# A four-layer graph network on one core: node tiles placed in mirrored order when the front half of the edge chunks meets more buckets, and a look-up list of 2080 entries in place of 3248

## The chip, the core and the metric

The program runs on one core of one Trainium2 chip. The metric is the device time of one execution in microseconds (us). A core has TensorE (PE in the profile; its weight loads are listed apart as PEld), VectorE (DVE), ScalarE (ACT), GpSimd (POOL) and SyncE (SP). Each engine has a sequencer that takes its instructions in the order in which they are written; in the profile a q behind the engine's name (PEldq, DVEq, ACTq, SPq) marks what the sequencer itself does: waits, register work, issue of DMAs. Matmuls write to PSUM, which has eight banks of 512 fp32 columns per partition.

## What is computed

Four graph layers run on 6250 nodes with 128 features and 200,000 edges. Each takes h = relu(layernorm(x)) and adds its result to x:

```python
x = x + gin(h, ...)      # sums of h[src] by dst, then two linear layers
x = x + gat(h, ...)      # attention over the edges
x = x + sage(h, ...)     # three times: mean of h[src] by dst
x = x + meta(h, ...)     # the edge layer, below

def meta(x, edge_index, edge_attr, u, batch, W1a, b1a, W1b, b1b, W2a, b2a, W2b, b2b):
    row, col = edge_index
    h = concatenate([x[row], edge_attr], axis=1)
    h = relu(h @ W1a + b1a) @ W1b + b1b
    sums = segment_sum(h, col, n_nodes)
    agg = sums / clip(counts, 1.0)[:, None]
    z = concatenate([x, agg, u[batch]], axis=1)
    return relu(z @ W2a + b2a) @ W2b + b2b
```

The edges come sorted by dst; src is random. Both are inputs, so the program counts and sorts them itself.

## The kernel before

**Sizes.** Nodes lie in 49 tiles of 128. A bucket is a pair (dst tile, src tile): 49 x 49 = 2401. Edges are stored by bucket in chunks of 128, two chunks to a pair; each dst tile begins at a new pair. There is room for 832 pairs, 1664 chunks. Counted from the inputs, 807 pairs are filled, and 25 lie empty at the end.

**Stages in order.** A histogram of the buckets; a chain of small steps that each wait for the one before (`relay`), which turns it into positions; `place_and_scatter`, which computes each edge's row and writes it to the tensor `bucketed` in HBM; `build_adjacency`, which makes the 49 x 49 blocks of the count matrix; the GIN, GAT and three SAGE layers, which multiply with that matrix; `edge_pass`, for the meta layer; and the tail.

**The edge pass** (6919 to 8991 us) has two blocks. It needs relu(table[src] + edge term) for every edge, `table` being the node part of the first linear layer, and sums it by dst. The chunks are treated in two ways. The far half (the last 416 pairs) is gathered from HBM by POOL with indirect DMAs (L2082), two per pair. The near half (the first 832 chunks) is looked up by TensorE from a copy of the table on chip: for every (chunk, src tile) that has edges, DVE makes a 128 x 128 one-hot matrix (L2220) and TensorE multiplies it with the tile of the table into the chunk's bank (L2161). This is one look-up. Both halves run interleaved in the first block: with each far pair go `PER_PAIR` = 8 look-ups. The list of look-ups has `LOOKS` = 3248 entries, a bound that holds for any graph; entries behind the last real look-up are dummies that add zeros to a bank nobody reads. Counted from the inputs, 3925 look-ups would serve all chunks, and 2021 of them fall in the near half.

**What sets the order in the first block.** DVE does per pair n: `message` (L2195), load of the chunk and tile numbers of the 8 look-ups into registers (L2210, L2212, TENSOR_LOAD), 8 one-hots (L2220), `rectify` (L2200), `add` for pair n-1 (L2206) and the scatter matrix of pair n+3 (L2188). TensorE's sequencer does per pair: the same two register loads (L2167, L2169), 8 look-ups (each a wait, two register operations, then the matmul, which is two weight loads and two matmuls in fp32), and the pair's own product (L2178), which waits for `rectify`. The one-hots have 8 buffers. ACT prepares each near chunk's bank with the edge term (`prepare`, L2114) and, when the chunk's look-ups are done, empties it with the relu (`evict`, L2121); there are four banks, so chunk c+4 is prepared after chunk c is emptied. After each four chunks ACT's sequencer issues three DMAs (L2145, L2098, L2103) and loads four registers (L2137). DVE waits for the bank (`s_clear`) at every second look-up. The second block (`near_pe`, L2274 and on) sums the near rows by dst and has no look-ups.

**The adjacency stage.** POOL reads `bucketed` back in 208 rounds of 8 chunks (L843, L847); every 16 rounds fill a chunk block, which TensorE turns (`turn`, L918); `find` (L927 to L930) picks the columns for 128 hits with selectors that DVE makes (L875), and the hits follow in runs of 16: DVE makes two one-hots each (L889, L890), TensorE multiplies (L942), ACT empties banks, SP stores blocks (L985).

## Time and profile before

| | us |
|---|---|
| median of 3 runs | 8997.42 (8996.03 to 9005.73) |
| the profiled execution | 9031.9 |
| its span | 9030.2 |

| engine | busy us | share | instructions |
|---|---|---|---|
| PE | 6296.6 | 70% | 36507 |
| PEld | 4249.3 | 47% | 36507 |
| DVE | 6360.5 | 70% | 17765 |
| ACT | 2836.5 | 31% | 6169 |
| POOL | 2691.6 | 30% | 2966 |

The shares are means over stages with different limits, so each stage has to be read by itself. PEclk is the clock that TensorE was granted: 1.00 is 2.4 GHz, 0.50 is 1.2 GHz. "Idle before" is what ended an engine's idle time; "issue" says that nothing in the profile shows what it waited for. A line number is that of the kernel's source.

### The profile page before, as it was taken

What the parts mean: (1) busy time and instruction counts of PE and PEld (TensorE: products, weight loads), DVE (VectorE), ACT (ScalarE), POOL (GpSimd) and SP (SyncE); (2) the same over time, 40 slices, a digit from 0 to 9 for tenths busy, and PEclk for the clock granted to TensorE, in tenths of its full rate; (3) what the DMA queues carried; (4) which work ended last, traced back from release to release, by engine and by line L of the source; (5) the groups of instructions that cost most, each with busy time, mean ns of one, the idle gap of its engine ahead of it and who ended that gap; (6) DMA issues with size and microseconds to landing.
All of it is one profiled execution on the core that took longest, in us unless ns stands there. A gap on an engine that the chain in (4) does not pass through costs nothing. (4 is left out here: it accounts for less than half of the span.)

```text
span 9030.2 us, 137943 instructions
## 1 busy us (share of the span) xinstructions
PE 6296.6 (70%) x36507; PEld 4249.3 (47%) x36507; DVE 6360.5 (70%) x17765; ACT 2836.5 (31%) x6169; POOL 2691.6 (30%) x2966
## 2 busy tenths in 40 slices
PE   4767777777555666566501788599997777777779
PEld 3545555555312222222201777444445666666668
DVE  6777777777668999655588999611024777777778
ACT  0222222222245776344400788300001333320000
POOL 0666767766646200000000000000002444444430
PEclk9666666666667999799855999799999999999999
DMA  2333333333498555699597666276676776752256
GB/s 98 94 96 95 97 97 97 96 97 97 127 393 270 163 169 145 227 337 329 163 387 311 207 215 213 95 245 217 215 251 178 180 183 179 181 144 63 63 105 194
DMA packets 1048196, 1605.78 MB, mean 178 GB/s; under 512 B 111567, under 2 KB 699236, under 8 KB 1033906
## 3 DMA queue, kind: packets, MB, share of 16 engines
q1 hardware_dynamic: 761756, 1179.89, 41.4%
q0 software_dynamic: 111328, 277.62, 9.5%
q10 hardware_dynamic: 174394, 139.51, 5.8%
q8 instruction: 351, 5.75, 0.3%
q14 instruction: 367, 3.01, 0.1%
HBM read 1177.49 MB, written 419.08 MB: 177 GB/s over the span
## 5 line engine op out<-in xcount | busy, mean ns | idle before, releaser
L774 POOL DMA_INDIRECT bucketed<-arena,wide x1563 | 1527.1, 977 | 882.6 <-issue 850.6
L2161 PE MATMUL psum<-wide,arena 128*128 x6496 | 1210.4, 329 | 397.5 <-DVE arena L2220 391.5
L2161 PEld LDWEIGHTS psum<-wide,arena 128*128 128x128 f32 x6496 | 989.2, 195 | 616.9 <-issue 491.8
L2220 DVE TENSOR_SCALAR arena<-wide,tile_first 128x128 f32 x3248 | 871.4, 302 | 469.4 <-PE psum L2161 289.8
L2082 POOL DMA_INDIRECT arena<-table,src_i x832 | 802.0, 964 | 1006.9 <-PE psum L2178 870.8
L942 PE MATMUL psum<-arena 128*128 128x512 bf16 x2304 | 705.8, 444 | 425.5 <-DVE arena L890 247.4
L662 PE MATMUL psum<-w_edge,arena 128*128 128x256 f32 x1568 | 869.7, 655 | 0.0
L890 DVE TENSOR_SCALAR arena<-sums 128x512 bf16<-128x512 int16 x2304 | 821.1, 356 | 0.0
L691 ACT CAST wide<-psum 49x49 f16<-49x49 f32 x1568 | 310.8, 198 | 1556.0 <-PE psum L669 893.9
L2030 POOL DMA_DIRECT2D table<-wide x13 | 9.6, 736 | 2478.5 <-DVE wide L1929 2478.5
L1686 PE MATMUL psum<-sums,arena 128*128 128x129 f32 x4802 | 602.3, 281 | 154.3 <-DVE arena L1676 154.3
L889 DVE TENSOR_SCALAR arena<-sums 128x128 bf16<-128x128 int16 x2304 | 599.3, 260 | 123.4 <-PE psum L942 122.3
L942 PEld LDWEIGHTS psum<-arena 128*128 128x128 bf16 x2304 | 241.2, 105 | 884.0 <-issue 723.8
L1686 PEld LDWEIGHTS psum<-sums,arena 128*128 128x128 f32 x4802 | 556.0, 192 | 200.7 <-DVE arena L1676 200.7
L1869 PE MATMUL psum<-arena,h 128*128 128x512 f16 (+1 forms) x2548 | 561.0, 371 | 43.9 <-DMA arena<-halved 42.4
L1370 DVE SCALAR_TENSOR_TENSOR arena<-arena 128x1536 f16<-128x1536 f32 (+2 forms) x245 | 359.0, 1465 | 312.6 <-ACT arena L1335 273.9
L669 PE MATMUL psum<-arena 128*113 128x177 bf16 x1568 | 546.4, 348 | 0.0
L968 ACT COPY wide<-psum 128x512 f32<-128x512 f32 x637 | 370.7, 582 | 472.3 <-PE psum L942 303.7
L1276 PE MATMUL psum<-arena,h 128*128 128x512 f16 (+1 forms) x1274 | 331.5, 398 | 248.7 <-ACT arena L1335 248.3
L1638 ACT ACTIVATE arena<-wide,s_a_mild 128x1280 f32<-128x1280 f32 (+1 forms) x245 | 326.8, 1334 | 439.8 <-PEq L103 439.8
L1335 ACT ACTIVATE arena<-arena 128x1536 f16<-128x1536 f32 (+2 forms) x245 | 305.6, 1248 | 434.9 <-DMA arena<-adjacency 415.0
L2121 ACT ACTIVATE arena<-psum 128x128 f32<-128x128 f32 x832 | 229.5, 276 | 670.1 <-PE psum L2161 562.6
(475 smaller groups left out, 12384.7 us busy)
## 6 DMA issues: line engine op xcount, KB each, us to landing
arena<-halved SPq DMA_DIRECT2D x441, 384.0 KB
arena<-adjacency SPq DMA_DIRECT2D x98, 1568.0 KB, 7.8
adjacency<-wide SPq DMA_DIRECT2D x588, 256.0 KB, 2.3
arena<-adjacency SPq DMA_DIRECT2D x196, 640.0 KB, 3.9
arena<-adjacency SPq DMA_DIRECT2D x147, 768.0 KB, 6.8
arena<-bucketed POOLq DMA_DIRECT2D x208, 528.0 KB, 6.1
halved<-arena SPq DMA_DIRECT2D x147, 384.0 KB, 6.3
wide<-bucketed ACTq DMA_DIRECT2D x208, 256.0 KB
```

The lines of the kernel that those rows point to most:

```text
L662: e.matmul(terms(k, c), lhsT=attr[k][:, at:at + P], rhs=W["edge"][:, :, :].rearrange("p c n -> p (c n)"), start=True, stop=True)
L669: update = e.matmul(psum[0:SPAN, 0, 0:TILES + P], lhsT=hot[k][:, c, by_dst], rhs=hot[k][:, c, by_both], start=False, stop=True, skip_group ...
L774: e.indirect_dma_start(bucketed, bass.IndirectOffsetOnAxis(ap=places[k][0:size, c:c + 1], axis=0), rows[k][0:size, c, :], None).then_inc(s ...
L889: e.tensor_scalar(hot_src[:, k, :], from_one[:, 0:P], row_of[:, ds(i * RUN + k, 1)], None, op0=ALU.is_equal)
L890: e.tensor_scalar(hot_key[:, k, :], from_one[:, 0:GROUP * P], key_of[:, ds(i * RUN + k, 1)], None, op0=ALU.is_equal).then_inc(s_ready, 1)
L942: e.matmul(flat[:, ds((bucket[k] & (BANKS - 1)) * 512, 512)], lhsT=hot_src[:, k, :], rhs=hot_key[:, k, :], start=False, stop=True, skip_gr ...
L968: e.copy(stage[:, k, :], psum[:, k, :]).then_inc(s_staged, 1)
L1686: last = e.matmul(psum[:, 4 * (r % 2) + c // 3, 129 * (c % 3):129 * (c % 3) + 129], lhsT=slots[n % 4][:, c * P:(c + 1) * P], rhs=node_rhs( ...
L1869: last = e.matmul(psum[:, 4 * (p % 2) + j, 0:width], lhsT=nodes[:, q, w, :], rhs=pieces[n % 4][:, 512 * j:512 * j + width], start=q == 0 a ...
L2082: e.indirect_dma_start(ring[:, k, c, :], None, table, bass.IndirectOffsetOnAxis(ap=src_i[:, chunk:chunk + 1], axis=0)).then_inc(s_got[k], 16)
L2161: e.matmul(flat[:, ds((chunk & 3) * 512 + 2048, P)], lhsT=hot[:, i % 8, :], rhs=table_in[:, ds(tile * P, P)], start=False, stop=True, skip ...
L2220: e.tensor_scalar(hot[:, i % 8, :], rows[:, ds((chunk[k] & 15) * P, P)], tile_first[:, ds(tile[k], 1)], None, op0=ALU.is_equal).then_inc(l ...
```

## The change

After the histogram, 35 more small steps count how many look-ups the near half would have. If it has more than half of all, tile t takes the place of tile 48 - t (`turn_round`, `swap`), and the empty pairs (`lead`, 25 here) lie ahead of the first edge instead of behind the last. The larger half is then far, and the list can be shorter for any graph: `LOOKS` is 2080, and `PER_PAIR` is 5, so all 416 far pairs carry look-ups (before 406). With the given inputs the comparison is 2 x 2021 > 3925, the tiles are mirrored, and the near half has 1906 look-ups; its first 50 chunks are empty. The counts are exact, since they are whole numbers made from the inputs.

Around this, `fill_spare` also blanks the first 112 chunks; `find` looks at one chunk block more, since the columns may lie up to 50 chunks later, so that two blocks are turned before the first `find`; SP reads the column of each block it stores from registers; ends of empty chunks are held at 1 or above.

```diff
-LOOKS = -(-(NEAR + BUCKETS_49 + 2) // 16) * 16
+MOST_LOOKS = (2 * (N_EDGES // (PAIR * P) + TILES) + BUCKETS_49 - TILES) // 2 + TILES
+LOOKS = -(-(MOST_LOOKS + 2) // 80) * 80
-PER_PAIR = 8
+PER_PAIR = 5
+LEAD = -(-2 * (PAIRS - N_EDGES // (PAIR * P)) // 16) * 16
...
             e.dma_start(bucketed_v[:, SPARE:CHUNKS, :]...).then_inc(s_empty, 16)
+            e.dma_start(bucketed_v[:, 0:LEAD, :].rearrange("p (r c) w -> p r (c w)", c=16),
+                        empty.rearrange("p c w -> p (c w)").unsqueeze(1).broadcast_to([P, LEAD // 16, 16 * EDGE_ROW])
+                        ).then_inc(s_empty, 16)
...
-                e.wait_ge(s_empty, 16)
+                e.wait_ge(s_empty, 32)
...
+        which_half = [
...
+            ("vector", lambda e, _: e.scalar_tensor_tensor(turn_round, both_sums[:, 1:2], 2.0, both_sums[:, 0:1], ALU.mult, ALU.is_gt), 1),
+            ("vector", lambda e, _: e.tensor_tensor(lead, lead, turn_round, ALU.mult), 1),
...
+            ("vector", lambda e, _: e.tensor_scalar(swap, iota[0:TILES, 0:TILES], row_to, None, op0=ALU.is_equal), 1),
...
+            ("tensor", lambda e, _: e.matmul(psum[0:TILES, 1, 0:TILES], lhsT=swap, rhs=hist, start=True, stop=True), 1),
+            ("vector", lambda e, _: e.tensor_copy(hist, psum[0:TILES, 1, 0:TILES]), 1),
+        ]
+        positions = which_half + [
...
             def chunk_blocks(b):
-                return [m for m in range(b - LAG, b + 1) if 0 <= m < CHUNK_BLOCKS]
+                return [m for m in range(b - LAG, b + 2) if 0 <= m < CHUNK_BLOCKS]
...
                     turn(0)
+                    turn(1)
                     find(0)
                     for b in range(BLOCKS):
                         batches(b, 0, 2)
                         if b + 1 < BLOCKS:
-                            turn(b + 1)
+                            turn(b + 2)
...
                     def store_blocks(i, rows):
+                        _, column = nc.values_load_multi_w_load_instructions(
+                            tile_column[:, i * BANKS:i * BANKS + rows], engines=(ENG.SP,), ...)
...
-                            e.dma_start(adj[:, g * GROUP:g * GROUP + w, ds(i * (BANKS * P) + (b // GROUPS) * P, P)],
+                            e.dma_start(adj[:, g * GROUP:g * GROUP + w, ds(column[b // GROUPS], P)],
...
                     e.sem_inc(s_clear, 15)
+                    e.sem_inc(s_looked, 1)
...
                             if k % 2 == 0:
-                                e.wait_ge(s_clear, chunk[k + 1])
-                                if i >= 8:
-                                    e.wait_ge(s_looked, i - 6)
+                                e.wait_ge(s_clear, chunk[min(k + 1, PER_PAIR - 1)])
+                                if i >= 7:
+                                    e.wait_ge(s_looked, i - 5)
```

DVE in the first block of the edge pass, the end of one pair. Before, the last two of eight look-ups share one wait, and `rectify` (L2200) follows:

```order
L2220 REGISTER_ALU [waits near_looked,near_clear]
L2220 ISA
L2220 TENSOR_SCALAR arena<-wide,tile_first 128x128
L2220 REGISTER_ALU
L2220 ISA
L2220 TENSOR_SCALAR arena<-wide,tile_first 128x128
L2200 TENSOR_SCALAR arena<-arena 128x256 [waits meta_sum]
```

Now the fifth and last look-up has a wait of its own, and `rectify` is L2260:

```order
L2280 REGISTER_ALU
L2280 ISA
L2280 TENSOR_SCALAR arena<-wide,tile_first 128x128
L2280 REGISTER_ALU [waits near_looked,near_clear]
L2280 ISA
L2280 TENSOR_SCALAR arena<-wide,tile_first 128x128
L2260 TENSOR_SCALAR arena<-arena 128x256 [waits meta_sum]
```

A pair has three one-hots fewer on DVE, and three look-ups fewer on TensorE, between the same neighbours; waits per pair go from four to three.

TensorE at the start of the adjacency stage. Before, one chunk block is turned (L918), then the first `find` (L927 to L930):

```order
L909 MATMUL psum<-blank 128x512 x4
L918 MATMUL psum<-ident,h 128x128 [waits s_cols]
L918 MATMUL psum<-ident,h 128x128 x2
L927 MATMUL psum<-wide 128x128 [waits s_picks]
L928 MATMUL psum<-wide 128x128
L930 MATMUL psum<-wide 128x128
L935 TENSOR_LOAD wide
```

Now two (L972), and `find` is L981 to L984:

```order
L963 MATMUL psum<-blank 128x512 x4
L972 MATMUL psum<-ident,h 128x128 [waits s_cols]
L972 MATMUL psum<-ident,h 128x128 x2
L972 MATMUL psum<-ident,h 128x128 [waits s_turned,s_cols]
L972 MATMUL psum<-ident,h 128x128 x2
L981 MATMUL psum<-wide 128x128 [waits s_picks]
L982 MATMUL psum<-wide 128x128
L981 MATMUL psum<-wide 128x128
L982 MATMUL psum<-wide 128x128
L984 MATMUL psum<-wide 128x128 x2
L989 TENSOR_LOAD wide
```

The first run of hits, behind the register load of L935 (now L989), stands behind a second wait for POOL's columns.

## Rows read from the trace of the kernel before

**Rows 1.** Two stretches: us, busy (xinstructions) of PE, PEld, DVE, ACT, POOL, PEclk, DMA, GB/s.

```profile
7300.00:7500.00 200.00, 156.34 (x899) 132.24 (x899) 145.60 (x538) 79.64 (x299) 85.03 (x91) 0.96 0.70 182
8300.00:8500.00 200.00, 159.31 (x946) 133.59 (x946) 151.29 (x567) 0.00 (x0) 90.45 (x94) 1.00 0.25 64
```

**Rows 2.** By line, 8100 to 8500 us: xcount | busy us, mean ns | idle before.

```profile
L2161 PE MATMUL psum<-wide,arena 128*128 x1514 | 277.2, 324 | 81.3 <-DVE arena L2220 80.9
...
L2220 DVE TENSOR_SCALAR arena<-wide,tile_first 128x128 f32 x757 | 200.3, 294 | 97.7 <-PE psum L2161 72.1 <-issue 10.6
L2082 POOL DMA_INDIRECT arena<-table,src_i x189 | 181.5, 961 | 218.2 <-PE psum L2178 188.9 <-issue 29.3
```

**Rows 3.** The same view, 7100 to 7500 us.

```profile
L2161 PE MATMUL psum<-wide,arena 128*128 x1427 | 267.1, 330 | 91.2 <-DVE arena L2220 89.2 <-issue 1.1
...
L2220 DVE TENSOR_SCALAR arena<-wide,tile_first 128x128 f32 x715 | 193.9, 306 | 109.1 <-PE psum L2161 60.8 <-ACT psum L2114 36.2 <-issue 4.9
```

**Rows 4.** Weight loads (PEld) in order of time: start us, us, what.

```profile
8305.06 0.53 PEld L2178 LDWEIGHTS psum<-arena 128*128 128x128 f32 x4
8306.64 2.67 PEld L2161 LDWEIGHTS psum<-wide,arena 128*128 128x128 f32 x16 [1.05 <-issue]
```

**Rows 5.** DVE in order of time, same columns, one pair.

```profile
8306.14 0.29 DVE L2200 TENSOR_SCALAR arena<-arena 128x256 f32<-128x256 f32 x1
...
8307.92 1.09 DVE L2220 TENSOR_SCALAR arena<-wide,tile_first 128x128 f32 x4 [0.62 <-PE psum L2161]
```

**Rows 6.** Register loads by line: xcount, ns min/median/max, first and last start.

```profile
L2167 PEldq TENSOR_LOAD <-wide x406: 587/592/1307, 6921.3 to 8711.9; - x136
...
L2137 ACTq TENSOR_LOAD <-src_i x208: 307/314/657, 6928.7 to 8062.4; - x104
...
L935 PEldq TENSOR_LOAD <-wide x144: 1101/1560/3655, 2471.1 to 3624.5; - x144
```

**Rows 7.** ACT around the end of four chunks, in order of time.

```profile
7161.79 0.28 ACT L2121 ACTIVATE arena<-psum 128x128 f32<-128x128 f32 x1 [0.43 <-PE psum L2161]
...
7164.03 0.28 ACT L2121 ACTIVATE arena<-psum 128x128 f32<-128x128 f32 x1 [1.66 <-issue]
```

**Rows 8.** Weight loads in a stretch at the lower clock, in order of time.

```profile
7182.04 3.39 PEld L2161 LDWEIGHTS psum<-wide,arena 128*128 128x128 f32 x16 [1.71 <-issue]
...
7186.33 2.67 PEld L2161 LDWEIGHTS psum<-wide,arena 128*128 128x128 f32 x16
```

**Rows 9.** Lines of the edge pass: xcount, ns min/median/max, first and last start us.

```profile
L2220 DVE TENSOR_SCALAR arena<-wide,tile_first x3248: 272/286/529, 6932.4 to 8712.9; 128x128 f32 x192
...
L2121 ACT ACTIVATE arena<-psum x832: 268/277/278, 6934.3 to 8066.7; 128x128 f32<-128x128 f32 x167
...
L2206 DVE TENSOR_TENSOR h<-h,psum x416: 267/280/289, 6938.2 to 8731.7; 128x128 f32 x139
```

**Rows 10.** Column copies of the adjacency stage, the same columns.

```profile
L843 POOL COPY h<-arena x208: 221/236/535, 2445.7 to 2820.9; 128x24 f32<-128x24 f32 x104
```

**Rows 11.** POOL at the start of the adjacency stage, in order of time.

```profile
2445.67 0.22 POOL L843 COPY h<-arena 128x24 f32<-128x24 f32 x1 [1.96 <-DMA arena<-bucketed]
...
2447.02 0.24 POOL L843 COPY h<-arena 128x24 f32<-128x24 f32 x1
```

**Rows 12.** Rows by line, 2426 to 2822 us, then 2822 to 3632 us.

```profile
L942 PE MATMUL psum<-arena 128*128 128x512 bf16 x476 | 187.6, 553 | 147.1 <-ACT psum L970 118.3 <-DVE arena L890 27.5 <-issue 0.9
...
L942 PE MATMUL psum<-arena 128*128 128x512 bf16 x1828 | 518.1, 415 | 278.5 <-DVE arena L890 219.9 <-ACT psum L970 51.3 <-issue 4.2
```

**Rows 13.** The chain of small steps before the scatter, in order of time.

```profile
153.66 0.14 DVE L419 CAST wide<-wide 49x1 f32<-49x1 int32 x1
...
155.42 0.14 DVE L427 TENSOR_SCALAR wide<-wide 49x1 f32<-49x1 f32 x1
...
156.80 24.11 SPq L411 DMA_DIRECT2D bucketed<-sums  x28
...
180.96 0.77 SPq L510 DMA_DIRECT2D hit_ends<-wide  x1
```

More of the change, by code:

```diff
@@ L413, in fill_last @@
             return emit
-        positions = [
+        first_i, final_i, next_i = (spread49[k].bitcast(i32) for k in (1, 2, 3))
+        filled, looks, looks_in, looks_at, flag, more_in = (spread49[k] for k in (4, 5, 6, 7, 8, 9))
+        swap = spread49[10]
+        both_looks, both_sums = spread49[11][:, 0:2], spread49[11][:, 2:4]
+        turn_round, lead, mirror, row_to, column_by, column_from = (spread49[12][:, k:k + 1] for k in range(6))
+        tile_column = sb("tile_column", [1, TILES], i32)
+        which_half = [
             ("vector", hist_wait, 1),
@@ L420, in build @@
             ("tensor", lambda e, _: e.matmul(psum[0:TILES, 1, 0:1], lhsT=before[0:TILES, 0:TILES], rhs=n_pairs, start=True, stop=True), 1),
-            ("vector", lambda e, _: e.tensor_copy(pair_at, psum[0:TILES, 1, 0:1]), 1),
+            ("tensor", lambda e, _: e.matmul(psum[0:TILES, 2, 0:1], lhsT=ones[0:TILES, 0:TILES], rhs=n_pairs, start=True, stop=True), 1),
+            ("vector", lambda e, _: e.tensor_scalar(pair_at256, psum[0:TILES, 1, 0:1], float(PAIR * P), None, op0=ALU.mult), 1),
+            ("vector", lambda e, _: e.tensor_scalar(lead, psum[0:TILES, 2, 0:1], -1.0, float(PAIRS), op0=ALU.mult, op1=ALU.add), 1),
@@ new lines, in build @@
+            ("vector", lambda e, _: e.tensor_tensor_scan(incl, ones[0:TILES, 0:TILES], hist, 0.0, ALU.mult, ALU.add), 1),
+            ("vector", lambda e, _: e.tensor_scalar(ends, incl, pair_at256, None, op0=ALU.add), 1),
+            ("vector", lambda e, _: e.tensor_tensor(first_i, ends, hist, ALU.subtract), 1),
+            ("vector", lambda e, _: e.tensor_scalar(final_i, ends, -1.0, None, op0=ALU.add), 1),
+            ("vector", lambda e, _: e.tensor_single_scalar(first_i, first_i, 7, op=ALU.arith_shift_right), 1),
@@ new lines, in build @@
+            ("vector", lambda e, _: e.tensor_scalar(looks_at, final_i, float(NEAR - 1), 1.0, op0=ALU.min, op1=ALU.add), 1),
+            ("vector", lambda e, _: e.tensor_tensor(looks_at, looks_at, first_i, ALU.subtract), 1),
+            ("vector", lambda e, _: e.scalar_tensor_tensor(looks_at, looks_at, 0.0, filled, ALU.max, ALU.mult), 1),
+            ("vector", lambda e, _: e.tensor_reduce(both_looks[:, 1:2], looks_at, axis=AX.X, op=ALU.add), 1),
+            ("tensor", lambda e, _: e.matmul(psum[0:TILES, 1, 0:2], lhsT=ones[0:TILES, 0:TILES], rhs=both_looks, start=True, stop=True), 1),
@@ new lines, in build @@
+            ("vector", lambda e, _: e.tensor_single_scalar(tile_column[:, :], tile_column[:, :], 7, op=ALU.arith_shift_left), 1),
+            ("tensor", lambda e, _: e.matmul(psum[0:TILES, 1, 0:TILES], lhsT=swap, rhs=hist, start=True, stop=True), 1),
+            ("vector", lambda e, _: e.tensor_copy(hist, psum[0:TILES, 1, 0:TILES]), 1),
+        ]
+        positions = which_half + [
+            ("vector", lambda e, _: e.tensor_reduce(tot, hist, axis=AX.X, op=ALU.add), 1),
+            ("vector", lambda e, _: e.tensor_scalar(tot_i, tot, float(PAIR * P - 1), None, op0=ALU.add), 1),
+            ("vector", lambda e, _: e.tensor_single_scalar(tot_i, tot_i, 8, op=ALU.arith_shift_right), 1),
+            ("vector", lambda e, _: e.tensor_copy(n_pairs, tot_i), 1),
+            ("tensor", lambda e, _: e.matmul(psum[0:TILES, 1, 0:1], lhsT=before[0:TILES, 0:TILES], rhs=n_pairs, start=True, stop=True), 1),
+            ("vector", lambda e, _: e.tensor_scalar(pair_at, psum[0:TILES, 1, 0:1], lead, None, op0=ALU.add), 1),
@@ L814, in build_adjacency @@
             head = part(h, 0, 3 * CHUNKS).rearrange("p (w c) -> p w c", w=3)
-            picks = [part(wide2, 2 * HITS + 64 * m, 64).bitcast(bf16) for m in range(LAG + 1)]
+            picks = [part(wide2, 2 * HITS + 64 * m, 64).bitcast(bf16) for m in range(LAG + 2)]
             from_one = part(sums, 0, 256).bitcast(i16)
@@ L868, in turn_and_pick @@
                     def turn_and_pick(b):
[L869 to L871 removed]
+                        for m in ([0, 1] if b == 0 else [b + 1]):
+                            if m < CHUNK_BLOCKS:
+                                e.wait_ge(s_turn, m + 1)
+                                e.tensor_copy(turned[:, m, :, :].rearrange("p w n -> p (w n)"), psum[:, 4, 0:3 * P]).then_inc(s_turned, 1)
                         if b:
@@ L980, in store_blocks @@
                     def store_blocks(i, rows):
+                        _, column = nc.values_load_multi_w_load_instructions(
+                            tile_column[:, i * BANKS:i * BANKS + rows], engines=(ENG.SP,), min_val=0, max_val=(TILES - 1) * P,
+                            skip_runtime_bounds_check_because="first node of a tile, made by this program from the tile's number")
                         for b in range(rows * GROUPS):
```

40 lines of the change are left out of this document (27 added, 13 removed).

## The prediction

> **What bounds the kernel now.** I read the stages first, by the view that gives busy time per stretch, then the groups by line, the order in time, and single lines. The stage that the change cuts is the first block of the edge pass. Its first one-hot starts at 6932.4 us and its last `add` at 8731.7 [rows 9]: 1799.3 us, a fifth of the span. In two stretches of it, one with near chunks and one after the last of them, ACT is busy or not at all, and the DMA engines 0.70 or 0.25 [rows 1]; no engine is full in either, so something periodic sets the pace. The period follows from the one-hots: 757 in 400 us is 4.23 us for each pair of eight in the far-only stretch [rows 2], 715 in 400 us is 4.48 us in the near stretch [rows 3].
>
> The reader is to see the 4.23 us put together on TensorE: 16 weight loads for eight look-ups in 2.67 us, four for the pair's product in 0.53, and a gap of 1.05 us before the next look-up [rows 4], sum 4.25. The gap is "issue", and in it the sequencer loads the numbers of the next look-ups: 592 ns each [rows 6], two per pair. The idle time that the groups give to DVE's one-hot [rows 2] is the same gap: DVE is ahead and itself waits for TensorE. DVE's own chain is close behind: from `rectify` to the next pair's first one-hot 1.78 us [rows 5], mostly its two register loads, then eight one-hots at 0.27 us at least [rows 9]: 2.18; with a load of tile numbers in every eighth pair (0.6 / 8 = 0.07) 4.03 us. POOL needs two gathers of 0.96 us and two pauses of 29.3 us / 95, some 0.31 each [rows 2]: 2.54 us.
>
> **The steps in the first block.**
>
> Look-ups: five per pair, six weight loads fewer at 2.67 / 16 = 0.167: -1.00 us per pair on TensorE, and three one-hots, -0.82, on DVE.
>
> Register loads: five numbers each instead of eight. The rows have loads of four (L2137, 314 ns), of eight (L2167, 592) and of 16 (L935, 1101 at least) [rows 6], about 70 ns for each number, so five should take 0.38: -0.42 us for the two, on either engine. The bounds are no gain, and the four-number load's -0.56. I take -0.42, by the rows on both sides. The Trainium skill ("DMA: Bandwidth & Descriptors", Latency and other measured facts) gives a floor of about 600 ns for a `tensor_load`; the row of four numbers at 314 ns disagrees. By that rule the step would be worth nothing, which is a rival below.
>
> New floors: TensorE 4.23 - 1.00 - 0.42 = 2.81 us; DVE 1.36 + 5 x 0.27 + 0.07 = 2.78; POOL 2.54. Three chains now lie within 0.3 us, where TensorE had 0.2 on DVE and 1.7 on POOL.
>
> In the near stretch a pair took 0.25 us more. DVE waited 36.2 us for ACT's banks over 715 / 8 = 89 pairs, 0.41 each [rows 3]. With 5 look-ups, a pair meets 832 / 1906 x 5 = 2.18 chunks instead of 832 / 2021 x 8 = 3.29, so 0.27, and this no longer has cover on DVE: 2.78 + 0.27 = 3.05. TensorE with the same addition as before comes to 3.06. Two coupled chains with equal length and irregular waits lose something to each other; I add half of the 0.27 and take 3.20. The ends are 2.81 (all hidden) and 3.75 (below).
>
> Count: 1906 look-ups are 381.2 near pairs, 34.8 more carry dummies. 381.2 x 3.20 + 34.8 x 2.81 = 1317.6 us.
>
> Start: the 50 empty chunks now lie first. DVE's first one-hot waits for chunk 50's bank, which is prepared after chunk 46 is emptied, and DVE holds everything behind it: `rectify`, so TensorE's product, so POOL's buffers. ACT must walk through 46 evictions. The step over a boundary of four chunks takes 7164.03 - 7161.79 = 2.24 us [rows 7], the others twice a copy of about 0.27, 0.51 with the overlap, so 3 x 0.51 + 2.24 = 3.8 us for four chunks, and 11.5 x 3.8 = 43 us. Bounds: 25 if the boundaries were free, 62 at the near stretch's own 5.45 us for four chunks (4.48 x 4 / 3.29). The pairs without look-ups at the end (now none), which ran quicker, cost 3 us more at the very end at most. So the block takes 43 + 1318 + 3 = 1364 instead of 1799: -435.
>
> **The steps before it.** Positions: 35 more steps ahead of SP's fills. Seven steps, two of them through TensorE, take 155.42 - 153.66 = 1.76 us [rows 13], 0.25 each: +8.8. The five steps behind the fills are hidden: SP issues fills for 24.11 us and only then the list that the next stage waits for [rows 13]. The other fill, of 112 chunks, costs its issue, some +0.4; it lands long before it is waited for.
>
> Adjacency: the first `find` needs 16 more of POOL's rounds. Undisturbed, one takes 2447.02 - 2445.67 = 1.35 us [rows 11], so it comes 21.6 us later. But until the last round at 2820.9 [rows 10] loads and stores share the DMA engines: 192 rounds from 2467.3 on took 1.84 each, so 16 undisturbed rounds give back 16 x 0.49 = 7.8, and the rounds end at 2813. By then 434 hits are done (476 in 348 us, 0.731 each), not 476, and the other 1870 run at 808 / 1828 = 0.442 us [rows 12]: 827 us, end at 3640 instead of 3630, +10. Twelve more selectors on DVE, which sets the pace there, at about a 0.29 us one-hot: +3. The register work on SP costs nothing: its 49 x 13 = 637 stores in some 1150 us leave it idle. Bounds +5 and +25; I take +13.
>
> Sum: -435 + 8.8 + 0.4 + 13 = -413 us. The profiled execution took 9031.9 us, 34.5 more than the median 8997.42; the difference carries over, so 8997 - 413 = **8584 us** (profiled about 8619).
>
> **The clock.** In a stretch at the lower clock (0.5, 1.2 GHz) the 16 weight loads take 3.39 us, but the next look-ups follow without a gap, 7186.33 - 7182.04 = 4.29 us later [rows 8]: the register loads hide behind slower work, and the pair costs what it did. Now ten loads at 0.212 and a product of 0.90 make 3.02 us, more than 2.81: the clock begins to count. The Trainium skill ("TensorE: Matmul & The Clock Gate", HAM oscillation) says that regular waits between groups of matmuls throttle the clock again. Here the gap stays, with less work around it, but relative work (14 products per 2.81 us against 20 per 4.23) rises; the row of the far-only stretch shows 1.00 at 20 per 4.23, so I expect it held.
>
> **Rivals.**
> - Register loads do not shrink: 3.23 far, 3.48 near. 43 + 381.2 x 3.48 + 34.8 x 3.23 + 3 = 1485; -314 + 22 = -292: 8705 us. For: the bottom of the TENSOR_LOAD rows for eight is stiff at 587. Against: the rows of 4 and 16.
> - Each of ACT's boundaries shows: 2.24 - 0.51 = 1.73 us per four chunks, 0.94 per pair, 3.75 us near. 1573; -226 + 22: 8793 us. For: no cover on DVE. Against: eight buffers hold 4 us of look-ups.
> - The clock stays low: 3.02 far, 3.20 + 0.21 near. 1451; -326: 8671 us.
> - Everything hides behind TensorE's 2.81: 43 + 416 x 2.81 + 3 = 1215; -584 + 22: 8435 us.
> - The comparison does not fire: 2021 look-ups in 404.2 pairs, no empty chunks ahead; 1330; -469 + 22: 8550 us. Against: 2 x 2021 is above 3925.
> - Slower: DVE's wait for a bank covers the whole pair in three steps, and each pair falls on one of ACT's boundaries in full, 2.79 + 2.24 = 5.03 us. 2061; +262 + 22: 9281 us. It decides from a near pair of 4.29 us on. Against: a boundary comes once in 1.8 pairs, and before DVE lost 0.41 us to ACT, not 2.24.
>
> **How the numbers follow.** Forecast 0.50, loads unchanged 0.12, boundaries shown 0.11, low clock 0.08, all hidden 0.12, no mirroring 0.03, slower 0.04. The forecast's own range is 8510 to 8660. From 8470 to 8740 it takes in the unchanged loads and the low clock and half of the hidden case, and leaves out the boundaries and the slower case: two in ten. A measurement of this kernel tells 0.2%, 18 us, from no change. Only the slower case and what lies between it and 8793 can end there: faster 0.95, same 0.01, slower 0.04.
>
> **What would show it.** Register loads of L2227 and L2270 near 0.38 us; one-hots (L2280) x2080; pairs of 3.2 us while ACT works, 2.8 after; first one-hot some 43 us later after the block's start; the last hit of the adjacency stage about 20 us later than now; the clock above 0.9 in the block. It is wrong if DVE's waits for ACT rise above 0.5 us per pair, or POOL's gathers become what pairs wait for.

## The result and the profile after

The changed kernel is slower: **9091.78 us** (median of 4 runs, 9084.15 to 9104.1) against 8997.77 (4 runs, 8996.03 to 9005.73) of the kernel before beside it. The ratio is 1.0104, interval 1.0087 to 1.0122: about 1%, small but clear of the noise. The forecast was 8584, and faster. A run that lay more than 1.5% above the fastest of its kernel is left out of medians and ratios; there is one such run, in experiment 8.

The profiled execution took 9096.69 us (span 9095.0) where that of before took 9031.9: +64.8. The profile of before is of an execution 34 us above its median and that of the changed kernel of one 5 us above, so the differences between the two profiles below add up to 65 us, not to 94.

The two stretches of the edge pass's first block, in the view of busy time per stretch (us, then busy of PE, PEld, DVE, ACT, POOL with instructions, PEclk, DMA share, GB/s), one with near chunks and one behind the last of them:

```profile
7400.00:7800.00 400.00, 261.21 (x1281) 230.18 (x1280) 225.98 (x823) 103.49 (x382) 176.13 (x184) 0.75 0.52 139
8660.00:8790.00 130.00, 85.30 (x438) 74.35 (x437) 76.97 (x282) 0.00 (x0) 49.40 (x52) 0.80 0.20 52
```

Against [rows 1], in the near stretch TensorE, DVE and ACT are *less* busy (PE 65% instead of 78%, DVE 56% instead of 73%), POOL is about as busy (44% and 43%), the DMA share fell from 0.70 to 0.52, and the granted clock is 0.75 instead of 0.96. Something waits more. The groups by line for 7400 to 7800 us (xcount | busy us, mean ns | idle before):

```profile
L2221 PE MATMUL psum<-wide,arena 128*128 x913 | 199.1, 378 | 136.7 <-DVE arena L2280 116.7 <-issue 19.7
L2141 POOL DMA_INDIRECT arena<-table,src_i x184 | 176.5, 959 | 225.9 <-PE psum L2238 195.3 <-issue 30.5
L2221 PEld LDWEIGHTS psum<-wide,arena 128*128 128x128 f32 x912 | 166.6, 252 | 167.5 <-issue 158.4
L2280 DVE TENSOR_SCALAR arena<-wide,tile_first 128x128 f32 x459 | 126.1, 303 | 168.0 <-PE psum L2221 68.2 <-ACT psum L2173 68.0 <-issue 26.7
```

459 one-hots are 91.8 pairs in 400 us: **4.36 us** for a pair of five look-ups, where eight took 4.48 [rows 3]. Weight loads wait 158.4 us for "issue", 1.73 us per pair. In order of time, one pair of the far-only stretch and the start of the next (weight loads on TensorE, with DVE's one-hots between them):

```profile
8703.02 1.67 PEld L2221 LDWEIGHTS psum<-wide,arena 128*128 128x128 f32 x10 [2.35 <-issue]
...
8704.61 0.53 PEld L2238 LDWEIGHTS psum<-arena 128*128 128x128 f32 x4
...
8706.47 1.41 DVE L2280 TENSOR_SCALAR arena<-wide,tile_first 128x128 f32 x5 [1.69 <-issue]
...
8707.43 1.67 PEld L2221 LDWEIGHTS psum<-wide,arena 128*128 128x128 f32 x10 [2.30 <-issue]
```

The work is what was forecast: ten weight loads in 1.67 us (2.67 x 10 / 16) and a product in 0.53. The gap is not: 2.30 us where before it was 1.05 [rows 4]; the period is 8707.43 - 8703.02 = 4.41. What fills it are the register loads, by line with ns min/median/max (L2227 and L2229 TensorE, L2270 and L2272 DVE):

```profile
L2227 PEldq TENSOR_LOAD <-wide x416: 582/1235/2195, 6938.1 to 8792.2; - x139
...
L2229 PEldq TENSOR_LOAD <-arena x416: 582/1230/1988, 6938.7 to 8793.5; - x139
...
L2270 DVEq TENSOR_LOAD <-wide x416: 592/1184/1830, 6947.8 to 8790.5; - x139
...
L2272 DVEq TENSOR_LOAD <-arena x416: 582/1183/2118, 6948.4 to 8791.8; - x139
```

Five numbers take 1.23 us, twice what eight took [rows 6]. The shortest are 0.58, and they come at regular places. Four pairs in a row, L2229 in the same columns:

```profile
L2229 PEldq TENSOR_LOAD <-arena x1: 694/694/694, 8647.2 to 8647.2; - x1
...
L2229 PEldq TENSOR_LOAD <-arena x1: 1242/1242/1242, 8651.1 to 8651.1; - x1
...
L2229 PEldq TENSOR_LOAD <-arena x1: 1230/1230/1230, 8656.0 to 8656.0; - x1
...
L2229 PEldq TENSOR_LOAD <-arena x1: 1228/1228/1228, 8660.4 to 8660.4; - x1
```

In every fourth pair it is near 0.6 (583 and 590 ns in the next two such pairs), in the other three 1.23. Pair n's five numbers start at number 5n, which is a multiple of four (16 bytes) for every fourth n. 1.23 / 5 is 0.246 us for each number. The whole trace has the same order: of L2229's 416 loads the first of every four (start at a multiple of four) has a median of 0.590 us, and the others, which start one, two and three numbers behind such a multiple, 1.243, 1.230 and 1.230.

These rows show a second thing. Five numbers from a multiple of four took 0.59 us, what eight take [rows 6], and not the 0.38 that the prediction expected of five. So the length alone was priced wrong as well: the steps that the rows show are for four numbers (0.31 us), eight (0.59) and sixteen (1.10), and five cost as much as eight.

The profile of the kernel *before* has such lines too, which the prediction did not read: loads of seven and of thirteen numbers.

```profile
L407 SPq TENSOR_LOAD <-last_i x4: 1142/2264/2862, 155.5 to 174.0; - x4
L407 ACTq TENSOR_LOAD <-last_i x3: 1396/2877/2897, 160.9 to 174.1; - x3
...
L960 ACTq TENSOR_LOAD <-wide x49: 1018/3146/3952, 2441.0 to 3561.1; - x49
```

Thirteen numbers at a median of 3.15 us are 0.242 each, while sixteen from a multiple of sixteen took 1.10 at least [rows 6]. Loads of 7 and 13 at steps of 7 and 13 meet a multiple of four only once in four, as those of 5 do. Of the loads of thirteen every fourth took 1.02 to 1.61 us, the others 2.91 to 3.95. The loads of seven are few and point the same way only roughly: the two that start at a multiple of four took 1.14 and 1.40 us, the other five 1.74 to 2.90, where seven times 0.246 would be 1.72.

The other stages. The block's first one-hot and its last `add`, and the last eviction of a near chunk, as in [rows 9]:

```profile
L2280 DVE TENSOR_SCALAR arena<-wide,tile_first x2080: 273/286/528, 6988.8 to 8794.4; 128x128 f32 x190
...
L2180 ACT ACTIVATE arena<-psum x832: 270/278/280, 6945.9 to 8653.3; 128x128 f32<-128x128 f32 x167
...
L2266 DVE TENSOR_TENSOR h<-h,psum x416: 267/280/290, 6994.5 to 8798.6; 128x128 f32 x139
```

DVE at the start of the block, in order of time:

```profile
6947.74 0.42 DVE L2255 TENSOR_TENSOR arena<-arena 128x256 f32<-128x256 f32 x1 [3.93 <-DMA arena<-table,src_i]
6988.79 1.29 DVE L2280 TENSOR_SCALAR arena<-wide,tile_first 128x128 f32 x5 [40.62 <-ACT psum L2173]
```

The start costs 40.6 us, against 43 forecast. SP's issues at the very beginning, in order of time (first number the start, second the time the issue took):

```profile
43.36 0.42 SPq L304 DMA_DIRECT2D bucketed<-sums  x1
43.83 0.56 SPq L307 DMA_DIRECT2D bucketed<-sums  x1
44.43 13.39 SPq L310 DMA_DIRECT2D look_marks<-blank  x1
57.86 2.54 SPq L311 DMA_DIRECT2D chunk_marks<-blank  x1
```

The second fill (L307) costs 0.56 us to issue, as forecast, but the third DMA stands 13.39 us behind the two. Only then do SP and the casts of DVE go on, and the histogram starts at 68.1 us instead of 54.6. Lines of the adjacency stage and of POOL's column copies (the latter in [rows 10] before), and the scatter before it:

```profile
L827 POOL DMA_INDIRECT bucketed<-arena,wide x1563: 909/958/1208, 269.8 to 2439.4; - x196
...
L944 DVE TENSOR_SCALAR arena<-sums x2304: 333/344/4580, 2514.7 to 3665.7; 128x512 bf16<-128x512 int16 x192
...
L896 POOL COPY h<-arena x208: 222/236/569, 2461.1 to 2834.7; 128x24 f32<-128x24 f32 x104
```

Before, the same scatter ran from 246.4 to 2423.9 and the same hits from 2472.5 to 3629.9. So the delay against before is +23.4 us where the scatter starts, +15.5 where it ends, +35.8 at the last hit, +66.9 at the block's last `add` (8731.7 before), +64.8 at the end.

### The profile page after: what moved, and what is told of

It is laid out like the page before. It is cut to its first block and busy times, and to the rows that moved or that the text cites. A ratio compares the mean times of both kernels' runs of the same rounds, so it can differ in the third digit from the quotient of the medians.

```text
span 9095.0 us, 127306 instructions
## 1 busy us (share of the span) xinstructions
PE 6057.6 (67%) x34166; PEld 4109.2 (45%) x34219; DVE 6070.1 (67%) x16644; ACT 2844.1 (31%) x6169; POOL 2693.8 (30%) x2966
## 5 line engine op out<-in xcount | busy, mean ns | idle before, releaser
L2221 PE MATMUL psum<-wide,arena 128*128 x4160 | 907.4, 378 | 674.1 <-DVE arena L2280 598.6
L2221 PEld LDWEIGHTS psum<-wide,arena 128*128 128x128 f32 x4160 | 760.6, 253 | 815.0 <-issue 773.1
L2280 DVE TENSOR_SCALAR arena<-wide,tile_first 128x128 f32 x2080 | 569.9, 301 | 794.4 <-ACT psum L2173 328.1
L944 DVE TENSOR_SCALAR arena<-sums 128x512 bf16<-128x512 int16 x2304 | 799.4, 347 | 0.0
L943 DVE TENSOR_SCALAR arena<-sums 128x128 bf16<-128x128 int16 x2304 | 577.0, 250 | 119.7 <-PE psum L996 119.0
```

The source lines that it names most:

```text
L943: e.tensor_scalar(hot_src[:, k, :], from_one[:, 0:P], row_of[:, ds(i * RUN + k, 1)], None, op0=ALU.is_equal)
L944: e.tensor_scalar(hot_key[:, k, :], from_one[:, 0:GROUP * P], key_of[:, ds(i * RUN + k, 1)], None, op0=ALU.is_equal).then_inc(s_ready, 1)
L2221: e.matmul(flat[:, ds((chunk & 3) * 512 + 2048, P)], lhsT=hot[:, i % 8, :], rhs=table_in[:, ds(tile * P, P)], start=False, stop=True, skip ...
L2280: e.tensor_scalar(hot[:, i % 8, :], rows[:, ds((chunk[k] & 15) * P, P)], tile_first[:, ds(tile[k], 1)], None, op0=ALU.is_equal).then_inc(l ...
```

## The experiments

**Theory:** a register load costs what the rows of 4, 8 and 16 numbers show (0.31, 0.59, 1.10 us) only if its first number lies at a multiple of four; otherwise each number costs about 0.24 us (0.246 on TensorE, 0.237 on DVE, where five took 1.18). **Rivals:** the loads are slow because five is an odd count; or they are slow because the loop around them is, and the real loss is ACT's banks after the mirroring.

Where not said otherwise runs are from one chip on which the kernel before took 9003.95 us (7 runs); on two others it took 9611.67 and 9622.74, since the scatter runs slower there (2710 to 2800 us from its first to its last part instead of 2178), so each ratio is to runs of before taken beside it.

**1. Aligned loads in the changed kernel.** Same look-ups, loads of eight numbers from the multiple of four at or below 5n:

```
- here = slice(n * PER_PAIR, (n + 1) * PER_PAIR)
+ here = slice(n * PER_PAIR // 4 * 4, n * PER_PAIR // 4 * 4 + 8)
- look_up(n * PER_PAIR + k, chunk[k], tile[k])
+ look_up(n * PER_PAIR + k, chunk[n * PER_PAIR % 4 + k], tile[n * PER_PAIR % 4 + k])
```

> The changed kernel, but each register load of a pair's look-up numbers begins at a multiple of four numbers (16 bytes) and reads eight, of which five are used. Theory (start of the load): in the changed kernel a load of five took 0.59 us in every fourth pair, where it began at such a multiple, and 1.23 us in the other three; here all take 0.59. TensorE's floor per pair is then 4.23 - 1.00 = 3.23 us, near 3.5 to 3.6, far 3.25: block 43 + 381 x 3.55 + 35 x 3.25 = 1510 us instead of 1810, total about 8790 us, clock in the block back above 0.9. Rival (with five look-ups per pair ACT's bank boundaries and the low clock set the pace, the loads fill idle time): the total stays within 50 us of 9090.

Measured: **8672.69 us** (8669.75 to 8676.74), ratio 0.9633 (0.9617 to 0.9649): 419 us less than the changed kernel. Loads by line, then the stretch 7300 to 7700 us with near chunks and one behind the last of them, and the groups in the first:

```profile
L2227 PEldq TENSOR_LOAD <-wide x416: 587/591/1381, 6926.2 to 8369.4; - x139
```

```profile
7300.00:7700.00 400.00, 285.75 (x1664) 240.01 (x1662) 292.84 (x1070) 132.15 (x488) 229.05 (x238) 0.96 0.68 179
8280.00:8370.00 90.00, 65.14 (x392) 54.12 (x392) 67.16 (x248) 0.00 (x0) 41.79 (x44) 1.00 0.23 63
```

```profile
L2221 PE MATMUL psum<-wide,arena 128*128 x1188 | 229.5, 332 | 114.2 <-DVE arena L2281 104.6 <-issue 8.9
...
L2281 DVE TENSOR_SCALAR arena<-wide,tile_first 128x128 f32 x595 | 163.8, 304 | 103.1 <-PE psum L2221 70.2 <-ACT psum L2173 19.1 <-issue 7.8
```

595 / 5 = 119 pairs: **3.36 us** each, 1.00 less, with the mirroring and its empty chunks still in place. Theory: three loads of 1.23 and one of 0.59 average 1.07, 0.48 more than 0.59; two per pair are 0.96, times 416 = 400 us. 419 were measured. The 8790 expected were 117 us too many: the expectation set a new block with its start in it (1510) against an old one without it (1810), and priced a near pair at 3.55 us where 3.37 came, (8260.5 - 6976.6) / 381.2. DVE's wait for ACT's banks fell from 68.0 / 91.8 = 0.74 us per pair to 19.1 / 119 = 0.16, so it was a consequence. The clock was one too: 0.75 went to 0.96 in the near stretch and 0.80 to 1.00 in the far one. Of the 1.00 us, (199.1 + 80.8) / 91.8 - (229.5 + 77.1) / 119 = 0.47 is TensorE's busy time, at the lower clock before (80.8 and 77.1 are its product, L2238, in the two stretches) and 136.7 / 91.8 - 114.2 / 119 = 0.53 its idle time. The two together are one cause seen twice: with the loads short, both go.

**2. The kernel before with both lists one number later.** Eight look-ups and loads of eight, nothing of the change, but each list starts 4 bytes further on. The two parts behind the list in `wide` move up by 16 numbers (64 bytes), which is not shown:

```
- tile_of = room(LOOKS).bitcast(i32)[0:1, :]
- chunk_of = part(wide, 0, LOOKS).bitcast(i32)[0:1, :]
+ tile_of = room(LOOKS + 16)[:, 1:LOOKS + 1].bitcast(i32)[0:1, :]
+ chunk_of = part(wide, 1, LOOKS).bitcast(i32)[0:1, :]
```

> The kernel before, with both look-up lists placed one number (4 bytes) later on chip, so that every load of eight numbers begins off a 16-byte multiple; all else the same. Theory (start of the load): each number is then fetched by itself at 1.23 / 5 = 0.25 us, a load of eight takes 1.97 us instead of 0.59, 2.76 us more per pair on TensorE's and DVE's sequencers, 406 pairs: total about 10,100 us. Rival (an odd count of five is what is slow, or the contention of the denser loop, not the start): loads stay at 0.59 us and the total at 9000 us.

Measured: **10114.2 us** (2 runs, 10112.66 and 10115.75; expected about 10,100), ratio 1.1233 (1.1211 to 1.1256). TensorE's load, by line:

```profile
L2167 PEldq TENSOR_LOAD <-wide x406: 1930/1936/2630, 6902.0 to 9790.4; - x136
```

The odd count is out: the same even loads go from 0.592 [rows 6] to 1.94 us, 0.242 per number, by their place alone. Two of them per pair are 2.69 us more; 1110 us over 406 pairs are 2.73. The granted clock in 7300 to 7700 us was 0.67 here, with eight look-ups per pair as before, so it fell without a change in the matmuls.

**3. The kernel before with both lists two numbers later** (8 bytes), one run. The edit is that of experiment 2 with 2 in place of 1.

> The kernel before with both lists two numbers (8 bytes) later instead of one. If only a start at 16 bytes lets a load take several numbers at once: loads of eight at 1.9 us and about 10,110 us, as e2_shifted. If a start at 8 bytes is enough for steps of two numbers: four steps, about 1.1 us, total about 9,400 us. If 8 bytes are enough for full steps: 0.59 us, 9,000 us.

Measured: 10704.33 us (one run) where before took 9611.67 there, 1.114. TensorE's load, by line:

```profile
L2167 PEldq TENSOR_LOAD <-wide x406: 726/1936/2721, 7485.0 to 10378.7; - x136
```

Eight bytes are not enough: the same median as four bytes. The changed kernel's loads that start two numbers behind a multiple of four say the same (1.230 us, above). Only the second load of either list on TensorE was short, 0.73 and 0.71 us; why stays open.

**4. No mirroring.** The kernel of experiment 1 with the comparison forced false, so tiles stay in order, no empty chunks lie first, and 2021 look-ups meet the near chunks instead of 1906:

```
- e.scalar_tensor_tensor(turn_round, both_sums[:, 1:2], 2.0, both_sums[:, 0:1], ALU.mult, ALU.is_gt)
+ e.scalar_tensor_tensor(turn_round, both_sums[:, 1:2], 0.0, both_sums[:, 0:1], ALU.mult, ALU.is_gt)
```

> e1_aligned with the comparison forced to false: tiles keep their order, no empty chunks ahead, 2021 look-ups in the near half (the list of 2080 still holds them); all added steps stay. Theory: the wait for ACT at the start of the edge pass (40.62 us in the changed kernel) goes, and 23 pairs more are near pairs at 0.3 us each: 41 - 7 = 34 us less than e1_aligned. Rival (mirroring is worth more, since it takes 115 look-ups off the near half and ACT's pace sets the end): as slow as e1_aligned or slower.

Measured: 8658.04 us (8647.58 to 8668.47), ratio 0.9616 (0.96 to 0.9632). That is 14.6 below experiment 1, where 34 were expected; the intervals of the two ratios overlap, so which is faster is not settled. The evictions and the last `add`:

```profile
L2180 ACT ACTIVATE arena<-psum x832: 270/278/281, 6947.6 to 8323.1; 128x128 f32<-128x128 f32 x167
...
L2266 DVE TENSOR_TENSOR h<-h,psum x416: 267/279/289, 6950.2 to 8360.6; 128x128 f32 x139
```

Experiment 1 had its last eviction at 8260.5 and its last `add` at 8373.5. Mirroring ends ACT's part 63 us sooner and the block 13 us later. All 416 pairs make five look-ups, real or dummy, so 115 fewer real ones only turn near pairs (3.36 us) into far ones, which took 90 us / 28 = 3.21 in experiment 1 (392 matmuls of 14 per pair between 8280 and 8370 us). 23 pairs by 0.15 are 3.5 us, against the 40 at the start. So the block should be 36 us shorter without mirroring. Between the first register load and the last `add` it is 20.7 us shorter (1426.6 against 1447.3), and it starts 7.8 us later, in stages that the edit does not touch. What took the other 16 shows in the near pairs: 3.41 us, (8323.1 - 6945.6) / 404.2, against 3.37 in experiment 1, over 404 pairs. Why they are longer was not looked into.

**5. The kernel before with 2080 look-ups**, five per pair and aligned loads of eight, without positions, fill and mirroring of the change, but with its waits of DVE for five look-ups. It covers inputs with at most 2080 look-ups (here 2021), not any graph:

```
- LOOKS = -(-(NEAR + BUCKETS_49 + 2) // 16) * 16
+ LOOKS = 2080
- PER_PAIR = 8
+ PER_PAIR = 5
  (loads as in experiment 1, waits as in the changed kernel)
```

> The kernel before with the list at 2080 entries, five look-ups per pair and loads of eight that begin at a multiple of four; no mirroring and none of the steps, fills and blocks added for it. Theory: e3_no_mirror without the costs ahead of the edge pass, which the trace of the changed kernel gives as 13.5 us for the queue at the fill, 8.4 for the 35 steps and about 20 in the adjacency stage: 40 us less than e3_no_mirror, about 8715 us. If those 40 us are given back later, the same as e3_no_mirror.

Measured: **8614.83 us** (8603.47 to 8628.91), ratio 0.9572 (0.9556 to 0.9588), the fastest on this chip, and 43 below experiment 4 (40 were expected). Its lines for the scatter and the hits:

```profile
L774 POOL DMA_INDIRECT bucketed<-arena,wide x1563: 909/958/1209, 246.8 to 2414.9; - x196
...
L890 DVE TENSOR_SCALAR arena<-sums x2304: 333/344/1840, 2463.1 to 3622.0; 128x512 bf16<-128x512 int16 x192
```

From scatter's last to the first hit it has 48.2 us, as before (2472.5 - 2423.9 = 48.6); the changed kernel and experiment 4 have 75.3 and 75.6. So the change's overhead ahead of the block is there without any mirroring: 3660.4 (last hit of experiment 4) - 3622.0 = 38 us.

**6. One load of twelve numbers for two pairs**, in the kernel of experiment 5, and **7. one of twenty for four pairs**:

```
- if n * PER_PAIR < LOOKS:
-     here = slice(n * PER_PAIR // 4 * 4, n * PER_PAIR // 4 * 4 + 8)
+ if n % 2 == 0:                      (7: n % 4 == 0)
+     first = n * PER_PAIR // 4 * 4
      ... chunk_of[0:1, first:first + 12] ...   (7: first + 20)
```

> e4_before_short with the look-up numbers loaded once for two pairs: 12 numbers from a multiple of four on, twice per two pairs on TensorE and on DVE. At 0.07 us for each number such a load takes 0.86 us, 0.43 per pair instead of 0.59, so 0.32 us less per pair for the two lists. Theory (the sequencers' register loads are what each pair waits for): near pairs from 3.36 to about 3.05 us, 416 x 0.32 = 130 us less, about 8485 us. Rival (at 3.36 us the pairs are bound by ACT's banks or POOL's gathers): within 30 us of 8615.

> The same with one load of 20 numbers for four pairs: 1.43 us, 0.36 per pair and list, 0.46 us less per pair than e4_before_short. Theory: near pairs about 2.9 us, 190 us less than e4_before_short, about 8425 us. Rival (POOL, whose two gathers and pauses need 2.5 us per pair, or the burst of 2.9 us of loads in one pair of four empties TensorE's queue and the gain goes): no faster than e5_two_pairs.

Measured side by side on the second chip: 9246.19 us (6 runs), ratio 0.9601 (0.958 to 0.9622), and 9345.89 (4 runs), ratio 0.9715 (0.9681 to 0.975). The loads, of 6 and of 7:

```profile
L2167 PEldq TENSOR_LOAD <-wide x208: 690/849/1638, 7566.6 to 9002.0; - x104
```

```profile
L2167 PEldq TENSOR_LOAD <-wide x104: 1356/1694/2156, 7508.7 to 9046.2; - x104
```

0.85 us for twelve numbers fits 0.07 per number; 1.69 for twenty does not quite (1.36 at least). Neither expected gain came (130 us and 190 more). The load for four pairs made it worse: the block's one-hots take 9056.6 - 7521.1 = 1535 us with it and 9006.5 - 7578.0 = 1428 with one for two pairs, and the granted clock of 8000 to 8400 us was 0.75 in the one and 0.88 in the other. Experiment 5's kernel had not run on that chip, so 5 and 6 were run side by side on a third.

> The kernel before with 2080 look-ups and aligned loads of 8 numbers, once more on one chip with its rivals of two pairs per load. Expected 0.957 of before (0.9572 on the first chip), 50 to 60 us below the changed kernel with aligned loads.

> One load of 12 numbers for two pairs instead of one of 8 for each, beside the kernel it differs from by that alone. Theory A (what the loads save is given back, because DVE can run at most two PSUM banks ahead: a long pair with both loads, 4.3 us, follows a short one of 2.4): within 20 us of the kernel with a load for each pair. Theory B (the gain of 0.33 us a pair is real and was hidden by that other chip being slower): 100 to 130 us faster. If neither, and it is slower by 20 to 60 us, the lower granted clock (0.88 against 0.97 there) costs more than the loads give.

Measured: 9230.92 us (4 runs, 9228.29 to 9239.59), ratio 0.9601 (0.9568 to 0.9635), and 9218.94 (5 runs, 9173.26 to 9226.5), 0.9587 (0.9554 to 0.962): the same, as the first of the three cases of the expectation says. Experiment 5's kernel is 176 us below experiment 1's on this chip (9406.68, under 8), where 50 to 60 were expected and 58 came on the first chip; the two differ ahead of the block too, and where the rest comes from was not looked into. The block's one-hots take 8931.4 - 7506.1 = 1425 us and 8873.0 - 7443.8 = 1429. The groups of 8400 to 8800 us, first with a load per pair, then with one per two:

```profile
L2161 PE MATMUL psum<-wide,arena 128*128 x1182 | 226.2, 328 | 119.6 <-DVE arena L2221 95.2 <-issue 24.0
...
L2221 DVE TENSOR_SCALAR arena<-wide,tile_first 128x128 f32 x590 | 162.0, 305 | 105.5 <-PE psum L2161 42.7 <-issue 37.7 <-ACT psum L2114 19.0
L2178 PE MATMUL psum<-arena 128*128 128x128 f32 x472 | 74.5, 282 | 0.0
```

```profile
L2161 PE MATMUL psum<-wide,arena 128*128 x1179 | 232.9, 344 | 110.4 <-DVE arena L2226 71.8 <-issue 36.7
...
L2226 DVE TENSOR_SCALAR arena<-wide,tile_first 128x128 f32 x586 | 150.5, 298 | 115.7 <-issue 61.2 <-PE psum L2161 27.4 <-ACT psum L2114 20.7
L2179 PE MATMUL psum<-arena 128*128 128x128 f32 x472 | 83.2, 306 | 0.0
```

TensorE's idle time fell by 9 us and its busy time rose by 6.7 + 8.7 = 15 us; the granted clock was 0.98 in the one and 0.89 in the other. On DVE the waits for TensorE fell by 15 us and those for "issue" rose by 24: the two loads, 1.7 us together, now stand in one piece. One-hot groups there start at 8500.15, 8502.56 and 8506.03 us, a pair of 2.4 behind one of 3.5. That the time is the same is shown; what took the gain was not isolated. The two busy columns point at the lower clock; the expectation's own cause, that DVE runs at most two banks ahead so that a long pair follows a short one, fits the order of the one-hots and was not tested apart from it.

**8. The second fill issued later**, behind the loads of the weights, in the kernel of experiment 1. The lines of the L307 fill move from the function of the first fill to the end of the one that loads the weights. It was run on the second chip, and again on the third beside experiment 1:

> e1_aligned with the DMA that blanks the first 112 chunks issued behind the loads of the weights instead of ahead of the two small DMAs for the marks. Theory (in the changed kernel SP's queue stood 13.4 us at the first mark DMA, behind two fills of 7.4 MB): the histogram starts 13 us sooner and the total is 13 us less than e1_aligned. Rival: the queue stands at another DMA instead and the gain is given back, same as e1_aligned.

> The changed kernel with loads of 8 numbers from a multiple of 4, once more, as the measure for the three kernels beside it on the same chip. Expected ratio to before 0.963 if this chip is like the first one (0.9633 there); its histogram is to start at about 69 us and its third DMA issue of SP to take about 13.4 us, as there.

> The changed kernel with aligned loads, and with the second 7.4 MB fill issued behind the loads of the weights instead of ahead of the two fills of the mark tables. Theory A (the 13.5 us at the start are SP's third issue standing behind two large fills): histogram from about 54 us instead of 69, and the time 10 to 20 us below the kernel without that move. Theory B (the fill delays something else wherever it stands, so the 15 us come back in the scatter, which waits for it): no difference within 10 us.

Measured: 9360.83 us (3 runs, 9306.3 to 9422.2; a fourth took 9451.31), 0.9736 (0.9662 to 0.981), on the second chip; on the third 9282.4 (9271.41 to 9318.23), 0.9666 (0.9628 to 0.9704), and the kernel without the move 9406.68 (9328.11 to 9420.66), 0.9756 (0.9702 to 0.9809), where 0.963 had been expected from the first chip. SP's issues on the third chip, without the move and with it:

```profile
43.91 0.56 SPq L307 DMA_DIRECT2D bucketed<-sums  x1
44.51 13.38 SPq L310 DMA_DIRECT2D look_marks<-blank  x1
```

```profile
43.90 0.55 SPq L307 DMA_DIRECT2D look_marks<-blank  x1
44.50 1.14 SPq L308 DMA_DIRECT2D chunk_marks<-blank  x1
```

The wait of 13.4 us is gone, and the scatter starts at 254.2 us instead of 270.2: that part of the theory holds. The 124 us between the medians are another matter. In the two profiled executions 34 us of the difference are there when the scatter ends, 141 at the last hit of the adjacency stage. The scatter does not run evenly on that chip: its last part started at 3010.9 us in experiment 5's kernel and at 2958.3 in experiment 6's, which are the same up to there. So the worth of the move in the whole time is not settled; 15 us is what its mechanism gives at the place where it acts.

## Why the prediction was wrong

The step that failed is the one on register loads: "about 70 ns for each number, so five should take 0.38". Five took 1.23 us in three pairs of four and 0.59 in the fourth, 1.07 on average, so the two of a pair cost +0.96 us instead of -0.42. The rows it drew the line through (4, 8 and 16 numbers) all start at a multiple of four; the change moved the start to 5n, and the step priced the length alone. The line was wrong for five even so: from a multiple of four five numbers took the 0.59 us of eight, which is worth nothing. Of the 1.38 us between -0.42 and +0.96, 0.42 are the length and 0.96 the start. Its bounds, "no gain" and -0.56, had no loss in them: nothing excluded one, and the rows of 7 and 13 numbers in the same trace spoke for one.

With the measured size the prediction's own floor gives the far pair: TensorE 3.23 (its rival's far pair with unchanged loads) + 0.96 = 4.19 us, where the far pairs took 4.17 on average (the two shown, of the three in four with slow loads, are 4.41 apart). The near pairs took 4.37, 0.20 more, where 0.39 more had been forecast. So the sum needs no price for the lower clock (0.80 in the far stretch); what the clock and ACT's banks have in the 0.20 was not separated.

Experiment 1 is in effect the rival with unchanged loads, since its loads take 0.59 us: priced at 8705 us and given 0.12, it measured 8673.

- **Look-ups** (-1.00 us per pair on TensorE): right. Ten weight loads take 1.67 us, and experiment 1 has 3.21 us in the far stretch, where the rival with unchanged loads had 3.23.
- **Register loads:** wrong, above. Three different prices were open (0.59 us whatever the length, 70 ns per number, per-number loads at 246 ns) and the last was not among the cases. The Trainium skill ("DMA: Bandwidth & Descriptors", Latency and other measured facts) gives some 600 ns as a floor of such a load. The trace disagrees with it as a floor, since loads of four take 0.31 us; for five numbers from a multiple of four it comes out as measured, 0.59, and it says nothing of the start, from which the 1.23 come.
- **Near pair** (coupling, 0.39 us more than the far pair): too high, 4.37 - 4.17 = 0.20 in the changed kernel and 3.36 - 3.21 = 0.15 with aligned loads (its rival with loads of 0.59 had 0.25). DVE's wait for ACT is 0.16 us per pair in experiment 1; in the changed kernel it is 0.74, above the 0.5 that the prediction named as its own refutation.
- **Start of the block** (+43 us, bounds 25 to 62): right, 40.6.
- **Positions** (+8.8): right. `hit_ends` is issued at 202.94 us instead of 180.96 [rows 13]: +22.0, of which 13.5 were there at the histogram.
- **The other fill** (+0.4 us): wrong by its queue. Its own issue takes 0.56 us, but the next one waits 13.39 behind it. That queue was seen as only a cost of issue; what stands behind two large transfers on it was not asked. The scatter's end moved by 15.5 us instead of 9.2.
- **Adjacency** (+13 within the stage, 5 to 25): measured 35.8 - 15.5 = +20.3. The first hit came 53.6 us behind POOL's first column copy (2514.7 - 2461.1) instead of 26.8, so the 16 added rounds took 1.68 us each, not the 1.35 of [rows 11]: 26.8 instead of 21.6. The hits themselves then took 1151.0 us instead of 1157.4, 6.4 back where 8.6 had been reckoned with.
- **Clock** ("I expect it held"): wrong, 0.75 in the near stretch and 0.80 after it. Its reason (14 products per 2.81 us) rested on the failed step: at 4.36 us per pair the gaps are longer than before with less work between them, which is when the granted clock in these profiles fell (0.67 in experiment 2). With aligned loads it was 0.96 and 1.00. So the rule of the Trainium skill that regular waits between groups of matmuls throttle the clock again ("TensorE: Matmul & The Clock Gate", HAM oscillation), set aside in the prediction, agrees with these runs.

The forecast also let the 34.5 us between the profiled execution and the median of before carry over; in the changed kernel the two are 4.9 apart. In the profiled times, forecast -413 and measured +65, 478 apart: the block's first register load came at 6938.1 us instead of 6921.3 [rows 6], +16.8 where 22 had been forecast (of the +35.8 at the last adjacency hit, 19 came back in the stages between; why was not looked into). From there to the last `add` the block took +50.1 instead of -435, 485 more: 381.2 near pairs by 4.37 - 3.20 us are 446 (4.37 = (8653.3 - 6988.8) / 381.2), 34.8 far ones by 4.17 - 2.81 are 47 (4.17 = (8798.6 - 8653.3) / 34.8), the start -2; 491 in all. Both differences per pair are the loads' 1.38 us, less 0.02 in the far pair and less 0.21 in the near one, where the coupling had been taken too high.

The slower rival was priced at 9281 us and given 0.04; it is not what happened. Its place (ACT's banks) showed in the waits, but went with the loads in experiment 1. "It decides from a near pair of 4.29 us on" came true by another cause: the near pair measured 4.37, and the kernel is slower by 1%.

## What to carry to other kernels

When a change alters the stride or the start of something that was aligned by accident, price its start as well as its size: look for rows of the same instruction with odd lengths and steps before drawing a line through the even ones. Loads that run once per step should start at a multiple of 16 bytes, even if they then fetch numbers that nobody uses: eight for five cost 0.59 us, five cost 1.23. And when an engine's waits and its clock both get worse, remove the longest new gap first: here the clock and the waits for ACT came back by themselves. Padding a load with unused numbers has its limit: a load for two pairs gained nothing, and one for four cost 107 us in the block.

## What the runs showed of the hardware that was not expected

- A load of int32 numbers into registers from on-chip memory takes 0.31 us for 4, 0.59 for 5 and for 8, 0.85 for 12 and 1.10 for 16 (at least) if its start is a multiple of 16 bytes, and 0.23 to 0.25 us *per number* if the start is 4, 8 or 12 bytes off: 5 in 1.23, 8 in 1.94, 13 in 3.15, and on DVE 5 in 1.18 and 8 in 1.84.
- A third DMA on SP's queue took 13.4 us to issue behind two fills of `bucketed`; with one fill ahead of it the issue of the same DMA took 0.55.
- Fewer, longer loads (two of 0.85 us in every second pair instead of two of 0.59 in each) changed nothing in the time, and the granted clock fell from 0.98 to 0.89 beside them; two of 1.69 in every fourth pair made the block 107 us longer than those of 0.85, at 0.75 against 0.88.
